# Cross attention in a perceiver: transposes issued one step earlier, remainders subtracted in pieces by GpSimd, small vector work moved to ScalarE

## The chip, the cores and the metric

The kernel runs on one core of one Trainium2 chip. The time is the device time of one execution in microseconds. A core has TensorE (PE, with PEld as its weight load), VectorE (DVE), ScalarE (ACT), GpSimd (POOL) and SyncE (SP, which issues the DMAs); each works through its own queue in order and waits on semaphores.

## The reference, cut to what matters

The network has twelve stages on `x` of (2, 256, 256), that is 512 rows of 256. Stages 0, 3 and 6 are cross attentions with one head of width 256 against a context of (2, 4096, 256); the others (self attentions, feed forwards, and a 16-head cross attention as stage 9) are not touched.

```python
h = layernorm(x)
q = (h @ Wq + bq) * scale
scores = q @ (ctx @ Wk + bk).T          # stage 0: masked keys count as -inf
p = softmax(scores)                     # over 4096 keys
x = x + (p @ (ctx @ Wv + bv)) (@ Wo + bo in stage 0)
```

The kernel uses that `q Wk^T` can be formed once (512 x 256), so that scores are products with the context itself, and that the value weights can be applied after the mixing. `c = q . bk` is added to each row of scores.

## The kernel before, in words

`xattn(s, ...)` (L556 on) builds the programs of the four compute engines for the three cross attentions; `masked` is true for stage 0 alone, `project` too. The 512 rows are 4 tiles of 128 (`tile_of`), the 4096 keys of a batch are 4 parts of 1024, each part two chunks `k` of 512. A **step** `g` (0 to 15) is one tile against one part; its halves `h` are its two chunks. Steps `2j` and `2j+1` share their chunks, so a chunk is used by two steps one after the other.

The products keep the accuracy of float32 with three products of a narrower type: each operand is split into a head (`copy` to fp32r) and a remainder (operand minus head). What is split for every chunk:
- the transposed context: head `cth(k)` by ACT (`split_t`, L838), remainder `ctr(k)` by a subtraction (`rest_of_context`, L684) of 128 x 1024. `ctr_by_pool` says who does it: POOL for chunks 2 to 15 in stage 0, DVE for everything in stages 3 and 6;
- the context: head `cnh(k)` by ACT (`split_n`, L842), remainder `cnr(k)` by POOL (L897, 128 x 1024).

A step on TensorE: `score(g, h)` is 6 products of 512 columns (L163, in `mm`), `turn(g, h)` 4 transposes (L632) of the exponentials `P`, `mix(g, h)` 12 products of 256 columns (L163). The order is written out by hand: `turn(g,0)`, `score(g+2,0)`, `turn(g,1)`, `mix(g,0)`, `score(g+2,1)`, `mix(g,1)`; after step 13 the turns and mixes of steps 14 and 15, then the transposes of the result (L346, L347), the value product and the output product.

DVE in a step: in stage 0 `masked_scores` (L730: scores + c, min with a bound `MB` that `bound` builds from mask bytes, L722) for each half; `largest` (L737 a reduction over 1024 columns, then on 128 x 1 values L743/L746/L749 the running maximum, L753/L756 its negative `nb`, L758 the `gap` to the maximum before); `add_mixed` (L782, L785, L789); `sums` (L766 and, for a tile's last part, L770, L772, L774); `rest_of_weights` (L795: the transposed exponentials minus their head); in stages 3 and 6 `rest_of_context`.

ACT in a step: `head_of_weights(g, 0)` (L847), `exp(g+1)` (L852 on 128 x 1 from the gap, L854 on 1024 columns), `head_of_weights(g, 1)`, `split_t(g+4)`, `split_n(g+2)`.

POOL: in stages 3 and 6 first the key jobs of stage 9 (`job_pool`, L474 to L480, four instructions of 512 columns for one job; two jobs in `b3`, four in `b6`), then `split_t(2)`, `split_n(0)`, `split_t(3)`, `split_n(1)` (each `split_t` only where POOL has it), the jobs `t3`/`t6` (one each), `add_row_pool` (L364, four additions of 128 x 256), then for k from 2 on `split_t(k+2)`, `split_n(k)`.

Buffers: heads and remainders of the context rotate through 3, exponentials `P` through 2, `PTH`/`PTR` (transposed exponentials) through 3, the banks of the turns through 2 (`TR`; `TE`, with two banks of the scores, for steps 14 and 15).

At the start of a stage PE makes `q` (2 x 4 products), then `c` (24 products of one column in all with `bk`), then `q2 = Wk q` whose head `qnh` ACT takes (L871) and whose remainder `qnr` DVE (L709); `score(0, 0)` waits for `qnr` and `ctr(0)`.

## Time and profile before

| what | us |
| --- | --- |
| median of 3 runs (lowest, highest) | 1529.64 (1528.77, 1535.45) |
| the profiled execution, its own time | 1532.3 |
| its span in the profile | 1530.3 |
| busy: PE, DVE, ACT, POOL | 1439.8, 972.8, 739.3, 307.2 |
| mean granted clock of TensorE | 0.988 |

The span is the time from the first to the last instruction in the profile; the execution's own time is 2.0 us more. A granted clock of 1.0 is 2.4 GHz, 0.5 is 1.2 GHz. In the rows, a time at the left is the start in us from the span's start, the next number the duration; what stands in square brackets is the engine's idle time just before and what ended it. A row of windows has the stretch, its length, then the busy time of PE, PEld, DVE, ACT and POOL with the number of instructions, the granted clock, and DMA's share and GB/s. A busy PE row ends by a model, so start-to-start distances are used for TensorE. The three cross attentions lie at about 0 to 171, 383 to 519 and 610 to 747 us.

### The profile page before, as it was taken

To read this page: it belongs to the slowest core of one execution; us is meant where nothing else is said; L and a number is where in the kernel's file an instruction comes from. 1 tells how busy PE (TensorE), PEld (TensorE's weight loads), DVE (VectorE), ACT (ScalarE), POOL (GpSimd) and SP (SyncE) were. 2 spreads that over 40 slices of the span, in tenths; PEclk is the share of its full clock that TensorE was granted. 3 is DMA by queue.
4 is the path that set the end of the run, shared out by engine and by line. 5 is a ranking of instruction groups with operands and counts; after the bars stand their busy time and mean duration, and the time that the engine had idled before them with its cause. 6 is when DMAs were issued, how large, how long until landed. Compare 5 with 4: busy or idle time off the path is not lost.

```text
span 1530.3 us, 26042 instructions
## 1 busy us (share of the span) xinstructions
PE 1439.8 (94%) x10503; PEld 986.9 (64%) x10513; DVE 972.8 (64%) x1714; ACT 739.3 (48%) x1363; POOL 307.2 (20%) x253
## 2 busy tenths in 40 slices
PE   7888999999999899899899999999999899999998
PEld 4777574888688665689655544555555454555697
DVE  5787465454677454677454258889999892566533
ACT  3554333111566333566353246777777677315232
POOL 1665231000733040933202050110000000100000
PEclk9999999999999999999999999999999999999999
DMA  9311324221120520210313366654776611410140
GB/s 374 118 56 52 152 79 142 70 95 61 42 81 28 229 81 8 72 71 28 129 30 121 130 135 134 93 82 69 136 153 118 113 22 61 200 56 1 49 172 14
DMA packets 43005, 147.72 MB, mean 97 GB/s; under 512 B 6380, under 2 KB 21996, under 8 KB 34028
## 3 DMA queue, kind: packets, MB, share of 16 engines
q1 hardware_dynamic: 42888, 146.07, 33.2%
q8 instruction: 84, 1.38, 0.4%
q14 instruction: 33, 0.27, 0.1%
HBM read 123.49 MB, written 22.56 MB: 95 GB/s over the span
## 4 chain that ended last, share of the span: by engine, by line
PE 78%; DVE 9%; ACT 3%; issue 2%; ACTq 0%; DVEq 0%
PE PS L163 47%; PE PS L2363 8%; PE PS L2275 7%; PE PS L2260 5%; PE PS L1624 2%; PE PS L632 2%; DVE SM L2379 2%; PE PS L1853 1%; PE PS L1874 1%; DVE SM L737 1%; PE PS L2354 1%; PE PS L2949 1%; PE PS L1881 1%; PE PS L2854 1%; DVE AR L1068 0%
## 5 line engine op out<-in xcount | busy, mean ns | idle before, releaser
L2379 DVE TENSOR_REDUCE SM<-PS 128x1 f32<-128x1024 f32 x256 | 301.6, 1219 | 38.4 <-PE PS L2260 37.3
L163 PE MATMUL PS<-ARr 128*128 128x256 f32 (+1 forms) x672 | 172.8, 323 | 20.8 <-DVE ARr L795 11.1
L2275 PE MATMUL PS<-AR 49*128 49x256 bf16 (+1 forms) x1216 | 162.5, 271 | 1.1 <-DVE AR L2400 0.7
L163 PE MATMUL PS<-HT,AR 128*128 128x512 f32 x328 | 152.7, 613 | 2.5 <-ACT HT L355 1.6
L163 PE MATMUL PS<-CNr,ARr 128*128 128x256 f32 x672 | 129.5, 290 | 12.8 <-DVE ARr L795 8.1
L163 PEld LDWEIGHTS PS<-ARr 128*128 128x128 f32 x672 | 117.4, 194 | 35.4 <-issue 14.5
L163 PE MATMUL PS<-ARr,HTr 128*128 128x512 f32 x384 | 127.3, 413 | 4.1 <-DVE ARr L684 3.0
L2275 PE MATMUL PS<-AR,CT 49*128 49x256 bf16 (+1 forms) x832 | 124.2, 271 | 0.0
L163 PEld LDWEIGHTS PS<-CNr,ARr 128*128 128x128 f32 x672 | 103.0, 195 | 18.1 <-issue 8.2
L847 ACT CAST ARr<-PS 128x512 fp32r<-128x512 f32 x96 | 56.0, 583 | 121.4 <-PE PS L632 120.1
L163 PEld LDWEIGHTS PS<-HT,AR 128*128 128x128 f32 x328 | 61.1, 194 | 77.5 <-issue 73.6
L163 PE MATMUL PS<-AR 128*128 128x256 f32 (+3 forms) x504 | 109.7, 372 | 1.4 <-DVE AR L701 0.8
L2452 ACT ACTIVATE AR<-PS 128x512 f32<-128x512 f32 x172 | 93.5, 602 | 25.7 <-PE PS L2275 25.7
L2452 ACT ACTIVATE CT<-PS 128x512 f32<-128x512 f32 x168 | 91.5, 602 | 24.4 <-PE PS L2275 24.3
L163 PEld LDWEIGHTS PS<-AR 128*128 128x128 f32 x504 | 89.5, 190 | 19.2 <-issue 6.6
L474 POOL CAST CN<-CN 128x512 bf16<-128x512 f32 x32 | 20.3, 635 | 379.0 <-ACT HT L355 208.4
L2275 PEld LDWEIGHTS PS<-AR 49*128 49x128 bf16 (+1 forms) x1216 | 81.2, 94 | 20.2 <-issue 7.0
L163 PE MATMUL PS<-CT,CN 128*128 128x512 f32 (+1 forms) x256 | 89.8, 490 | 1.1 <-ACT AR L2465 1.1
L163 PE MATMUL PS<-CN,CT 128*128 128x256 f32 (+1 forms) x448 | 85.5, 340 | 2.4 <-DVE AR L1070 0.8
L897 POOL TENSOR_TENSOR CNr<-CN,ARr 128x1024 fp32r<-128x1024 f32 x30 | 70.3, 2344 | 70.3 <-ACT ARr L842 70.3
L163 PEld LDWEIGHTS PS<-CN,CT 128*128 128x128 f32 x448 | 70.5, 192 | 20.5 <-issue 10.3
L795 DVE TENSOR_TENSOR ARr<-PS,ARr 128x512 fp32r<-128x512 f32 x96 | 65.6, 687 | 25.5 <-ACT ARr L847 24.9
(397 smaller groups left out, 2708.6 us busy)
## 6 DMA issues: line engine op xcount, KB each, us to landing
CN<-ctx_n SPq DMA_DIRECT2D x24, 1024.0 KB, 5.0
AR<-k_parts SPq DMA_DIRECT2D x114, 128.0 KB
k_parts<-CN SPq DMA_DIRECT2D x32, 384.0 KB, 3.4
CT<-pack SPq DMA_DIRECT2D x6, 2048.0 KB, 8.0
AR<-pack SPq DMA_DIRECT2D x20, 512.0 KB, 4.6
CT<-k_parts SPq DMA_DIRECT2D x78, 128.0 KB
CT<-ctx_t SPq DMA_DIRECT2D x8, 1024.0 KB, 18.8
v_ones<-CN SPq DMA_DIRECT2D x28, 288.0 KB, 3.3
```

Source lines behind the costliest of these rows:

```text
L163: last = te.matmul(o, l, r, start=first and k == 0, stop=final and k == n - 1, skip_group_check=True)
L474: ge.tensor_copy(p[:, 0, :], r).then_inc(*pl.inc("split", "p0", 9, n))
L632: z = te.transpose(PS[:, b, tok(y)], P[g % 2][:, tok(4 * h + y)], ident)
L795: ve.tensor_tensor(PTR[u % 3], bank("pt", s, g, h), PTHf[u % 3], ALU.subtract).then_inc(*dv.inc("turn", "ptr", s, g, h))
L847: ae.copy(PTH[u % 3], bank("pt", s, g, h)).then_inc(*ac.inc("turn", "pth", s, g, h))
L897: pl.e.tensor_tensor(context_n(k, CNr), context_n(k, CN), CNHf[k % 3], ALU.subtract).then_inc(*pl.inc("rest", "cnr", s, k))
L1624: z = te.matmul(ACC[i], h[:, tok(i)], W[f"d{e}"], start=e == 0 and i % 2 == 0, stop=e == n - 1, skip_group_check=True)
L2260: return te.matmul(PS[:, b + y, :], QQ9[M_ROWS[e], pr, 0, tok(2 * b2 + g % 8 // 4)], KM9[g // 8 % 4][M_ROWS[e], c * 512:c * 512 + 512], st ...
L2275: return te.matmul(PS[:, b, z * 256:z * 256 + 256], keys[rows, c * 128:c * 128 + 128], QQ9[rows, pr, rest, cols], start=not rest, stop=boo ...
L2363: z = te.matmul(PS[32 * y:32 * y + 32, 7, 0:256], VP9[:, 2 * s + y % 2, 17 * h:17 * h + 32], PT9[n % 6][:, y, :], start=s == 0, stop=s == ...
L2379: ve.tensor_reduce(MX9[:, p % 2, e, g % 8 // 4, g % 4:g % 4 + 1], PS[:, b:b + 2, :].rearrange("p a b -> p (a b)"), AX, ALU.max).then_inc(* ...
L2452: ae.activation(PT9[i % 6][:, 2 * e:2 * e + 2, :], bank("st", 9, p, s, e).rearrange("p (c q) -> p c q", c=2), ACT.Exp).then_inc(*ac.inc("e ...
```

## The change

On TensorE, `turn(g+1, 0)` is issued ahead of `mix(g, 1)`, with the same order down to the last step, and the transposes of the result are issued tile by tile between the last mixes; in stages 3 and 6 the output products of tiles 0 and 1 stand ahead of the transposes of tile 3. The products `q2` come ahead of `c`. On DVE the running maximum is kept in an array `top`, so that in stage 0 it is a reduction over two neighbours instead of a two-operand maximum; the gap is gone, and ACT takes the exponential of the difference of the two maxima with its scale and bias. `bound` moves from DVE to ACT. `sums` moves behind `largest`. On ACT the context heads 0 and 1 are made ahead of `qnh`, and the order within a step is `head_of_weights(g, 1)`, `exp(g+1)`, `split_t(g+4)`, `bound(g+4)`, `head_of_weights(g+1, 0)`, `split_n(g+2)`. On POOL each subtraction of 1024 columns becomes four of 256, and `ctr(k)` for k from 2 on is POOL's in all three stages.

```diff
...
-        TE = banks.ring((4,), (5,), (0,), (2,))
+        OR = banks.ring((0,), (1,), (2,), (3,))
...
-            mxc, mx, nb, gap, al, rs, tot = (sm(16) for _ in range(7))
+            low = sm(1)
+            top = sm(4, 5, 2)
+            nb, al, rs, tot = (sm(16) for _ in range(4))
...
-            ctr_by_pool = lambda k: masked and k > 1
+            ctr_by_pool = lambda k: k > 1
...
+                for m in range(2):
+                    b, before = PB.take(("q2", s, m), ("qnr", s, m))
+                    pe.wait_ge(*before, ("qt", s, 0), ("qt", s, 1))
+                    mm(te, PS[:, b, :], [(Wk[:, h, tok(m)], QT[:, h, :]) for h in range(2)]).then_inc(
+                        *pe.inc("proj", "q2_ps", s, m))
                 b, before = PB.take(("c", s), ("cadd", s))
-                pe.wait_ge(*before, ("qt", s, 0), ("qt", s, 1))
+                pe.wait_ge(*before)
                 for i in range(4):
                     z = mm(te, PS[:, b, i:i + 1], [(QT[:, m, tok(i)], W["bk"][:, m:m + 1]) for m in range(2)])
                 z.then_inc(*pe.inc("proj", "c_ps", s))
-                for m in range(2):
-                    b, before = PB.take(("q2", s, m), ("qnr", s, m))
-                    pe.wait_ge(*before)
-                    mm(te, PS[:, b, :], [(Wk[:, h, tok(m)], QT[:, h, :]) for h in range(2)]).then_inc(
-                        *pe.inc("proj", "q2_ps", s, m))
                 if s:
                     half_pe(pe, f"h{s}", 1)
 
...
                 def turn(g, h):
-                    b, before = (TR if g < 14 else TE).take(("pt", s, g, h), ("ptr", s, g, h))
+                    b, before = TR.take(("pt", s, g, h), ("ptr", s, g, h))
                     pe.wait_ge(*before, ("e", s, g))
...
+                def turn_mixed(i):
+                    b, before = OR.take(("ot", s, i), ("ot", s, i))
+                    pe.wait_ge(*before, ("o", s, i))
+                    te.transpose(PS[:, b, 0:128], OB[:, i, 0:128], ident)
+                    te.transpose(PS[:, b, 128:256], OB[:, i, 128:256], ident).then_inc(*pe.inc("turned", "ot_ps", s, i))
+
...
                 for g in range(2):
                     score(g, 0)
                     score(g, 1)
-                for g in range(14):
-                    turn(g, 0)
-                    score(g + 2, 0)
+                turn(0, 0)
+                for g in range(16):
+                    if g < 14:
+                        score(g + 2, 0)
                     turn(g, 1)
                     mix(g, 0)
-                    score(g + 2, 1)
+                    if g < 14:
+                        score(g + 2, 1)
+                    if g < 15:
+                        turn(g + 1, 0)
+                    else:
+                        turn_mixed(0)
+                        turn_mixed(1)
                     mix(g, 1)
-                turn(14, 0)
-                turn(14, 1)
-                mix(14, 0)
-                turn(15, 0)
-                mix(14, 1)
-                turn(15, 1)
-                mix(15, 0)
-                mix(15, 1)
-                turn_all(pe, s, "ot", OB, "o")
-                src, Wf, ready = OT, Wv, [("ot", s, i) for i in range(4)]
+                turn_mixed(2)
                 if project:
+                    turn_mixed(3)
                     for m in range(2):
                         b, before = PB.take(("v", s, m), ("cx", s, m))
-                        pe.wait_ge(*before, *ready)
+                        pe.wait_ge(*before, *[("ot", s, i) for i in range(4)])
                         mm(te, PS[:, b, :], [(Wv[:, kt, tok(m)], OT[:, kt, :]) for kt in range(2)]).then_inc(
                             *pe.inc("proj", "v_ps", s, m))
-                    src, Wf, ready = CX, mat(W["Wo"], 2), [("cx", s, m) for m in range(2)]
-                for i in range(4):
-                    b, before = PB.take(("y", s, i), ("x", s, i))
-                    pe.wait_ge(*before, *ready)
-                    mm(te, PS[:, b, 0:256], [(src[:, kt, tok(i)], Wf[:, kt, :]) for kt in range(2)]).then_inc(
-                        *pe.inc("proj", "y_ps", s, i))
+                    for i in range(4):
+                        product(i, CX, mat(W["Wo"], 2), ("cx", s, 0), ("cx", s, 1))
+                else:
+                    product(0, OT, Wv, ("ot", s, 0))
+                    product(1, OT, Wv, ("ot", s, 1))
+                    turn_mixed(3)
+                    product(2, OT, Wv, ("ot", s, 2))
+                    product(3, OT, Wv, ("ot", s, 3))
                 pe.end(s)
 
...
                 pr.wait_ge(("cth", s, k))
-                pr.e.tensor_tensor(CTR[k % 3], context_t(k), CTHf[k % 3], ALU.subtract).then_inc(
-                    *pr.inc("rest", "ctr", s, k))
+                for kt, c in pieces or [(slice(0, 2), slice(0, 512))]:
+                    z = pr.e.tensor_tensor(CTR[k % 3][:, kt, c], context_t(k)[:, kt, c], CTHf[k % 3][:, kt, c],
+                                           ALU.subtract)
+                z.then_inc(*pr.inc("rest", "ctr", s, k))
...
-                if not masked:
+                if masked:
+                    ve.memset(low, -BIG).then_inc(*dv.inc("fill", "low"))
+                else:
                     rest_of_context(dv, 0)
...
-                dv.wait_ge(("c_ps", s))
-                ve.tensor_copy(cadd, bank("c", s)[:, 0:4]).then_inc(*dv.inc("proj", "cadd", s))
-                if not masked:
-                    rest_of_context(dv, 1)
+                if masked:
+                    rest_of_context(dv, 0)
+                rest_of_context(dv, 1)
                 for m in range(2):
                     dv.wait_ge(("qnh", s, m))
                     ve.tensor_tensor(QNR[:, m, :], bank("q2", s, m), QNHf[:, m, :], ALU.subtract).then_inc(
                         *dv.inc("proj", "qnr", s, m))
-                if masked:
-                    rest_of_context(dv, 0)
-                    rest_of_context(dv, 1)
-                else:
-                    rest_of_context(dv, 2)
-
-                def bound(g, h):
-
-                    k = chunk_of(g, h)
-                    c = slice(k % 8 * 512, k % 8 * 512 + 512)
-                    dv.wait_ge(("mu", g // 8), ("s", s, *last_use(k - 8)) if k > 7 else None)
-                    ve.tensor_scalar(MB[:, c], MU[g // 8][:, c], 2 * BIG, -BIG, ALU.mult, ALU.add).then_inc(
-                        *dv.inc("bound", "bound", k))
-
+                dv.wait_ge(("c_ps", s))
+                ve.tensor_copy(cadd, bank("c", s)[:, 0:4]).then_inc(*dv.inc("proj", "cadd", s))
...
-                            ve.scalar_tensor_tensor(out=of(mx, g), in0=of(mxc, g), scalar=c, in1=of(mx, g - 2), op0=ALU.add,
-                                                    op1=ALU.max).then_inc(*dv.inc("largest", "mx", s, g))
+                    ve.tensor_reduce(top[:, i, n, 1:2], P[g % 2] if masked else scores(g), AX, ALU.max).then_inc(
+                        *dv.inc("largest", "mxc", s, g))
+                    dv.wait_ge(("mxc", s, g), ("mx", s, g - 2) if n else None)
+                    if masked:
+                        ve.tensor_reduce(top[:, i, n + 1, 0:1], top[:, i, n, 0 if n else 1:2], AX, ALU.max).then_inc(
+                            *dv.inc("largest", "mx", s, g))
+                    elif n == 0:
+                        ve.tensor_scalar(top[:, i, 1, 0:1], top[:, i, 0, 1:2], c, None, ALU.add).then_inc(
+                            *dv.inc("largest", "mx", s, g))
+                    else:
+                        ve.scalar_tensor_tensor(out=top[:, i, n + 1, 0:1], in0=top[:, i, n, 1:2], scalar=c,
+                                                in1=top[:, i, n, 0:1], op0=ALU.add, op1=ALU.max).then_inc(
+                            *dv.inc("largest", "mx", s, g))
                     dv.wait_ge(("mx", s, g))
                     if masked:
...
-                    if not first:
-                        ve.tensor_tensor(of(gap, g), of(mx, g - 2), of(mx, g), ALU.subtract).then_inc(
-                            *dv.inc("largest", "gap", s, g))
+                        ve.tensor_tensor(of(nb, g), c, top[:, i, n + 1, 0:1], ALU.subtract).then_inc(
+                            *dv.inc("largest", "nb", s, g))
 
...
-                for g in range(16):
+                rest_of_weights(0, 0)
+                for g in range(15):
                     if g:
                         add_mixed(g - 1)
-                    sums(g)
-                    rest_of_weights(g, 0)
-                    if masked and g + 2 < 16:
+                    if masked and g < 14:
                         masked_scores(g + 2, 0)
                     rest_of_weights(g, 1)
                     if g + 4 < 16 and not ctr_by_pool(g + 4):
                         rest_of_context(dv, g + 4)
-                    if g + 2 < 16:
-                        if masked:
-                            masked_scores(g + 2, 1)
+                    if masked and g < 14:
+                        masked_scores(g + 2, 1)
+                    rest_of_weights(g + 1, 0)
+                    if g < 14:
                         largest(g + 2)
+                    sums(g + 1)
+                add_mixed(14)
+                rest_of_weights(15, 1)
...
                 add_mixed(15)
+                turn_mixed(2)
...
-                turn_out(dv, s, "ot", OT, 0)
...
-                    ac.wait_ge(("pt_ps", s, g, h), ("mix", s, (u - 3) // 2, (u - 3) % 2) if u > 2 else ("q2_ps", s, 1))
+                    ac.wait_ge(("pt_ps", s, g, h), ("mix", s, (u - 3) // 2, (u - 3) % 2) if u > 2 else ("c_ps", s))
...
-                        ac.wait_ge(("gap", s, g))
-                        ae.activation(of(al, g), of(gap, g), ACT.Exp).then_inc(*ac.inc("exp", "al", s, g))
+                    i, n = tile_of(g), part_of(g)
+                    if n:
+                        ac.wait_ge(("mx", s, g))
+                        ae.activation(of(al, g), top[:, i, n + 1, 0:1], ACT.Exp, scale=-1.0, bias=top[:, i, n, 0:1]).then_inc(
+                            *ac.inc("exp", "al", s, g))
                     ac.wait_ge(("nb", s, g), ("pt_ps", s, g - 2, 1) if g > 1 else None)
...
+                def bound(k):
+
+                    c = slice(k % 8 * 512, k % 8 * 512 + 512)
+                    ac.wait_ge(("mu", k // 8), ("low",), ("s", s, *last_use(k - 8)) if k > 7 else None)
+                    ae.activation(MB[:, c], MU[k // 8][:, c], ACT.Identity, scale=2 * BIG, bias=low).then_inc(
+                        *ac.inc("bound", "bound", k))
...
+                split_t(0)
+                split_t(1)
                 if s:
-                    split_t(0)
-                    split_t(1)
...
-                    for k in range(3):
-                        split_t(k)
+                    for k in range(4):
+                        bound(k)
+                    split_t(2)
                 split_n(0)
-                split_n(1)
                 exp(0)
                 split_t(3)
-                for g in range(16):
-                    head_of_weights(g, 0)
-                    if g + 1 < 16:
-                        exp(g + 1)
+                split_n(1)
+                head_of_weights(0, 0)
+                for g in range(15):
                     head_of_weights(g, 1)
+                    exp(g + 1)
                     if g + 4 < 16:
                         split_t(g + 4)
+                        if masked:
+                            bound(g + 4)
+                    head_of_weights(g + 1, 0)
                     if g + 2 < 16:
                         split_n(g + 2)
-                turn_out(ac, s, "ot", OT, 1)
+                head_of_weights(15, 1)
+                turn_mixed(1)
+                turn_mixed(3)
                 end_act(ac, s)
 
...
-                    pl.e.tensor_tensor(context_n(k, CNr), context_n(k, CN), CNHf[k % 3], ALU.subtract).then_inc(
-                        *pl.inc("rest", "cnr", s, k))
+                    for y in range(4):
+                        z = pl.e.tensor_tensor(context_n(k, CNr)[:, y, :], context_n(k, CN)[:, y, :], CNHf[k % 3][:, y, :],
+                                               ALU.subtract)
+                    z.then_inc(*pl.inc("rest", "cnr", s, k))
 
                 def split_t(k):
                     if ctr_by_pool(k):
-                        rest_of_context(pl, k)
+                        rest_of_context(pl, k, *[(kt, c) for kt in range(2) for c in (slice(0, 256), slice(256, 512))])
...
```

In the parts left out, `largest` writes the raw maximum of part n to `top[:, i, n, 1]`, `product` is the old output product, and `turn_mixed` on DVE and ACT is the old copy of the transposed result for one tile.

## Rows read from the trace of the kernel before

**Rows 1.** Windows from turn(0,0) or turn(2,0) to turn(14,0) in stages 0, 3, 6

```profile
36.50:148.18 111.68, 95.74 (x614) 84.79 (x613) 87.89 (x150) 58.71 (x94) 69.36 (x32) 0.97 0.19 68
419.60:499.95 80.35, 79.48 (x527) 70.93 (x525) 60.91 (x108) 49.96 (x80) 28.74 (x13) 1.00 0.16 54
648.70:728.66 79.96, 78.92 (x523) 70.76 (x521) 59.23 (x108) 49.08 (x80) 25.78 (x13) 1.00 0.17 56
```

**Rows 2.** Chain that ended last, stage 0, one step (start, us, what)

```profile
126.21 1.53 DVE SM L746
```

**Rows 3.** Groups of instructions by form, 44 to 149 us

```profile
L847 ACT CAST ARr<-PS 128x512 fp32r<-128x512 f32 x27 | 15.6, 576 | 33.4 <-PE PS L632 33.3
...
L746 DVE TENSOR_TENSOR SM<-SM 128x1 f32<-128x1 f32 x11 | 13.2, 1199 | 0.4
...
L722 DVE TENSOR_SCALAR CN<-CN 128x512 bf16<-128x512 uint8 x12 | 6.5, 545 | 0.0
```

**Rows 4.** Timeline, stage 0, POOL, DVE and PE around 44 to 50 us

```profile
44.19 2.38 POOL L684 TENSOR_TENSOR ARr<-CT,ARr 128x1024 fp32r<-128x1024 f32 x1
...
44.67 1.91 DVE L746 TENSOR_TENSOR SM<-SM 128x1 f32<-128x1 f32 x1
...
46.52 2.34 POOL L897 TENSOR_TENSOR CNr<-CN,ARr 128x1024 fp32r<-128x1024 f32 x1
...
46.69 2.19 DVE L758 TENSOR_TENSOR SM<-SM 128x1 f32<-128x1 f32 x1
...
49.86 2.93 PE L163 MATMUL PS<-CNr,ARr 128*128 128x256 f32 x12 [3.60 <-DVE ARr L795]
```

**Rows 5.** Timeline of PE, stage 3: a mix, and the second transposes behind it

```profile
431.10 1.59 PE L163 MATMUL PS<-CNr,ARr 128*128 128x256 f32 x12
...
434.35 0.60 PE L632 MATMUL PS<-CST,AR 128*128 128x128 f32 x4
```

**Rows 6.** Timeline, start of stage 0

```profile
17.59 5.49 PE L163 MATMUL PS<-AR 128*128 128x1 f32 x24 [0.84 <-DVE AR L701]
...
26.05 1.19 PE L163 MATMUL PS<-ARr,HTr 128*128 128x512 f32 x2 [2.97 <-DVE ARr L684]
...
26.95 2.61 DVE L722 TENSOR_SCALAR CN<-CN 128x512 bf16<-128x512 uint8 x1
...
35.74 1.11 PE L632 MATMUL PS<-CST,AR 128*128 128x128 f32 x4 [2.60 <-ACT AR L854]
```

**Rows 7.** DMA issues from 2.6 to 2.7 us (last number: us to landing)

```profile
CT<-ctx_t SPq DMA_DIRECT2D x1, 1024.0 KB, 10.6
```

**Rows 8.** PE after step 13, stage 3, with a window inside, then stage 0

```profile
503.12 0.37 PE L163 MATMUL PS<-ARr 128*128 128x256 f32 x1 [2.14 <-issue]
...
504.00:505.00 1.00, 1.00 (x7) 1.00 (x6) 0.00 (x0) 0.00 (x0) 0.00 (x0) 0.50 0.99 418
...
510.37 0.35 PE L163 MATMUL PS<-ARr 128*128 128x256 f32 x1 [1.74 <-DVE ARr L795]
...
515.01 3.69 PE L163 MATMUL PS<-AR,HT 128*128 128x256 f32 x16 [0.55 <-ACT HT L355]
...
163.29 3.67 PE L163 MATMUL PS<-HT,AR 128*128 128x512 f32 x8 [0.55 <-ACT HT L355]
...
167.80 3.72 PE L163 MATMUL PS<-AR,H 128*128 128x256 f32 x16 [0.85 <-DVE H L827]
```

**Rows 9.** Timeline of POOL (one of ACT) at the start of stages 0, 3, 6

```profile
41.63 2.59 POOL L364 TENSOR_TENSOR X<-X,AR 128x256 f32<-128x256 f32 x4
...
402.64 0.61 POOL L474 CAST CN<-CN 128x512 bf16<-128x512 f32 x1 [0.16 <-POOL CNr L897]
...
403.64 1.03 ACT L838 CAST ARr<-CT 128x1024 fp32r<-128x1024 f32 x1
...
407.25 3.86 POOL L364 TENSOR_TENSOR X<-X,AR 128x256 f32<-128x256 f32 x4
...
630.98 2.38 POOL L897 TENSOR_TENSOR CNr<-CN,CNr 128x1024 fp32r<-128x1024 f32 x1
```

37 lines of the change are left out of this document (18 added, 19 removed).

## The prediction

> **What bounds the kernel now.** I read the page first, then windows over the three cross attentions, because nothing outside them is edited. From turn to turn a step takes 111.68/14 = 7.98 us in stage 0, but 80.35/12 = 6.70 in stage 3 and about 6.7 in stage 6 [rows 1]. TensorE's work is the same in all three. From the start of a mix to that of the second set of transposes behind it (a mix, a set and a score, no gap) 434.35 - 431.10 = 3.25 us pass, and that is half a step: 6.50 [rows 5]. I work with **6.53**, split by columns: a score (6 x 512) 1.39, a mix (12 x 256) 1.41, transposes (4 x 128) 0.47 where they stand clear. So stage 0 has 1.45 us a step to give, stages 3 and 6 only 0.17.
>
> Who takes it in stage 0 is in the chain: DVE's running maximum on 128 x 1 values (L746) stands in it, with 1.53 us in the step shown [rows 2]. Over the loop it takes 1.20 on average, for one element a partition, [rows 3]. The timeline shows why: POOL starts a subtraction at 44.19 that ends at 46.57, and DVE's two-operand instruction from 44.67 ends at 46.58. The next one starts at 46.69 and ends at 48.88, with POOL's next subtraction, which ends at 48.86; TensorE then stands 3.60 us [rows 4]. A DVE instruction with two operands in SBUF waits for the whole POOL instruction in flight. The bound from bytes (L722), one operand of 512 columns, suffers the same: 2.61 us at the start, 0.55 on average [rows 3, 6].
>
> **Part 1, the loop of stage 0.** The new order puts turn(g+1,0) ahead of mix(g,1). Call T the start of a step on TensorE: score(g+2,0) to T+1.39, turn(g,1) to 1.86, mix(g,0) to 3.27, score(g+2,1) to 4.66, turn(g+1,0) to 5.13, mix(g,1) to 6.53. The wait that is added is turn(g+1,0)'s for exp(g+1), and mix(g,1) is queued behind it. ACT: head(g,1) ends at about 2.65, the exponential with its small one 4.04; due at 4.66, so 0.6 to spare. Then the transposed head (5.0), bound (5.5), head(g+1,0) (6.1). DVE: remainder 6.7, reduction 8.0, maximum and negative 8.4, which is T'+1.9 in the next step, ahead of ACT's 2.65 there. DVE's sums and the addition of the mix end by T'+3.2 even with one 0.65 wait, the second remainder at 4.6, due at 5.13. The loop closes on TensorE with 0.5 to spare.
>
> Loads: DVE had 87.89 us in 14 steps; without L746 and L722 it is 68.2, 4.9 a step, plus a reduction of two elements [rows 1, 3]. ACT had 4.2 a step and gets bound; nothing shows that on ACT, the nearest is its 512-column copy, 0.58 [rows 3]; below nothing is excluded, above I keep 1.1. That makes 4.8. POOL had 69.36/14 = 4.95; four 256-column additions took 2.59, so a unit of four pieces is 2.6 to 2.7 against 2.38 whole, and two units 5.4 a step [rows 1, 4, 9]. The upper end is 3.86 for such a four, while DVE was using the same side [rows 9]. All under 6.53. I price a step at **6.60**, between 6.53 and the 6.70 of stage 3.
>
> **Part 2, the start of stage 0.** q2 now follows qt directly, at 17.6, and c (1.9 us of one-column products within the 5.49 of the row) comes behind it [rows 6]. q2 ends at 21.05 and c at 22.95; both remainders are done by 22.6. The context heads 0 and 1 go ahead of qnh on ACT's queue, but the first 1 MB, issued at 2.7, lands at 13.3, in ACT's idle time: cost nothing; if it were after 19.5 it would hold qnh up one for one [rows 7]. The first score moves from 26.05 to 23.0. Four scores end at 28.6 at full clock (before they began at half clock after a 2.97 idle). The bounds, on ACT from 21.8 to 24.2, no longer stop DVE for 2.61. exp(0) ends at 29.5, turn(0,0) starts at 29.6 against 35.74 [rows 6]. Step 0 then waits 0.9 for head and remainder, so step 1 starts at 37.6 (37.5 on the side of POOL: cnr(1) 36.1). Step 14: 37.6 + 13 x 6.60 = 123.4. Before it is 148.18 + 0.47 = 148.65. **-25.2.**
>
> **Part 3, the loops of stages 3 and 6.** ctr(k) leaves DVE, which doesn't bind there. On POOL it is a second unit of 2.7. In steady state 5.4 of 6.6 is enough, and ctr(g+4) is ready 1.8 us before its score. But POOL starts with a debt. In stage 3, ctr(3) can't start before the head at 403.7; then come ctr(3), cnr(1), the job (402.64 to 407.25, 4.6), the row additions (2.7), ctr(4), cnr(2), ctr(5), cnr(3): 6 units, 403.7 + 16.2 + 4.6 + 2.7 = 427.2 [rows 9]. mix(2,1) needs cnr(3), so step 3 starts at 428.6 where TensorE could be at 423.9. Step 14: 428.6 + 11 x 6.60 = 501.2, against 499.95 + 0.47 = 500.4 [rows 1]: **+0.8.** In stage 6 four jobs hold POOL until 630.98; ctr(2), which DVE made beside them, now stands first, and with cnr(0), ctr(3), cnr(1), the row additions, ctr(4), cnr(2), ctr(5), cnr(3) it makes nine units, beside a job: 631.0 + 24.3 + 4.6 = 659.9, step 3 at 661.3, step 14 at 733.9 against 729.1 [rows 1, 9]: **+4.8.** ctr(2) at 633.7 keeps score(2,0) waiting some 3 us there; that lies inside this sum. The 0.6 us won at each start by c behind q2 is lost in the debt.
>
> **Part 4, the ends.** Before, from the end of turn(14,0) TensorE stood 2.14 us, ran three us at half clock (1.2 GHz granted in the window from 504), stood 1.74, mixed until 513.3, transposed four tiles, stood 0.55 and made the products until 518.6: 18.2 us from 500.4 [rows 8]. Now: turn(14,1), mix(14,0) to T+1.9; turn(15,0) waits for exp(15) until 3.3 and ends 3.8; mix(14,1) 5.2, turn(15,1) 5.7, mix(15,0) 7.1, two tiles' transposes 7.5, mix(15,1) 9.0 (its remainder is there at 7.6), tile 2 at 9.25, two products of 0.92 to 11.1, tile 3 11.35, products to 13.2. **-5.0** in stage 3 and, with the same shape, in stage 6. In stage 0, 22.75 (to 171.4) becomes 9.2 + 1.6 + the 8.1 of value and output products = 18.9: **-3.9** [rows 8]. A 1.4 us stall remains where there was 2.14; the clock fell after the 2.14 and not after the 1.74, so I count full clock. The bound on the other side is 1.3 each.
>
> **Sum.** -25.2 + 0.8 + 4.8 - 5.0 - 5.0 - 3.9 = -33.5 against the profiled execution's own 1532.3: 1498.8. That execution stands 2.7 above the median of 1529.64, so the median to expect is **1496**.
>
> Two rules beside it. GpSimd's subtraction of 1024 columns took 2.38 [rows 4]. The Trainium skill (GPSIMD Engine Reference, 3.1 Elementwise) gives 4.5 us for 2048 columns, which as an estimate is 0.56 for a 256 piece; with it the 16 units of debt would come to some 7 us less and the sum to 1489; the row has 2.38 for half of that and wins. The skill (Perfetto Trace Analysis, Optimizing Scalar/DVE Operations) also warns that moving work between these two engines may not help since they share a port; that speaks against part 3 and is rival C below.
>
> **The rivals.**
> A. *The debt is larger.* If the pieces stretch to the 3.86 per four that the row additions took beside DVE [rows 9], but only while POOL works without a break, each of 16 units costs 1.2 more: +19, 1515. Halfway, 1506. For it: DVE's small two-operand work is still there in stages 3 and 6. Against: the 2.59 of stage 0.
> B. *The turned-ahead wait binds.* If bound on ACT or a late maximum eats more than the 0.6, by say 0.5, stage 0 pays 14 x 0.5 = 7: 1503.
> C. *The pieces don't give way.* If DVE has to let all four pieces pass, it waits 2.6 for L766 and, in stages 3 and 6, up to three times; steps go back to about 7.9 in stage 0 and the gain is what ends and start give, 14 + 6, less the debt: about 1520 to 1528. Against: DVE got in at 46.58 between two POOL instructions that followed each other [rows 4]. The Trainium skill (SBUF, State Buffer, SBUF: two separate sides) gives the port to whoever starts first for a whole instruction, which leaves open who is first after a piece.
> D. *Slower.* POOL becomes the bound in all three loops. It decides above 6.6/8 = 0.825 us a piece; at the 0.96 of 3.86/4 a step takes 7.72, 1.12 more for 13 + 11 + 11 steps, +39, with A's 19: 1554.
> E. *Better.* Steps at 6.53 and a piece of 0.6: -2.5 - 4: 1489.
>
> **How the numbers follow.** Forecast 0.58, A 0.17, B 0.09, C 0.05, D 0.03, E 0.08. The range from 1487 to 1510 holds the forecast, E, B and half of A. Half a per cent, about what can be told here, is 7.6 us: faster means under 1522. C is half in that band: faster 0.93, same 0.04, slower 0.03.
>
> **What would show it.** Steps of stage 0 at 6.5 to 6.7 start to start, no DVE instruction on 128 x 1 above 0.8, a POOL piece of 0.65; turn(0,0) near 30; in stages 3 and 6 TensorE waiting in step 2 for POOL's L684 and L897, in stage 6 also ahead of score(2,0), and 6.6 afterwards; the end of each stage about 13 us (stage 0: 19) from the last score's step. It is wrong if TensorE waits for L854 in every step, or if POOL has no gap left by step 8.

## The result, and the profile after

The changed kernel takes **1511.24 us** (median of 4 runs, 1508.56 to 1514.65) against 1532.21 for the kernel before on the same chip (a fourth run moved its median from the 1529.64 of the table): ratio **0.9865**, 95% interval 0.9831 to 0.9898. It is faster, by 21 us or 1.35%, clear of the spread of the runs. The forecast was a fall of 33.5 us to 1496, and the time lies above its range, which ended at 1510. The profiled execution took 1511.16 with a span of 1509.4, 20.9 less than the 1530.3 before.

In the changed kernel the lines have moved: L700 and L929 are POOL's remainders of the transposed and the plain context, L364 the row additions, L747 the masked maximum of two values, L753 and L761 the unmasked maximum and its negative, L769 the running sum of the softmax, L634 the transposes of the weights, L798 their remainder.

Where the 20.9 us come from is read at landmarks: instructions on TensorE or ACT that stand at the same place in both programs. First the kernel before: the first value product after stage 0, ACT's copies ahead of the queries of stages 3 and 6, the first transposes of stage 4, the first product of stage 7, the last wait near the end.

```profile
384.49 0.63 ACT L355 COPY HT<-PS 128x256 f32<-128x256 f32 x2
540.40 0.33 PE L346 MATMUL PS<-CST,AR 128*128 128x128 f32 x1 [0.42 <-ACT AR L1515]
611.89 0.63 ACT L355 COPY HT<-PS 128x256 f32<-128x256 f32 x2
755.59 7.11 PE L163 MATMUL PS<-HT,AR 128*128 128x512 f32 x16 [0.43 <-ACT HT L355]
1522.06 1.13 PE L2946 MATMUL PS<-CN 128*128 128x256 f32 x4 [1.13 <-ACT CN L3180]
```

The same in the changed kernel, with its end of stage 0 (before: 163.29, [rows 8]):

```profile
142.63 3.67 PE L163 MATMUL PS<-HT,AR 128*128 128x512 f32 x8 [0.55 <-ACT HT L886]
363.07 0.63 ACT L355 COPY HT<-PS 128x256 f32<-128x256 f32 x2
515.61 0.33 PE L346 MATMUL PS<-CST,AR 128*128 128x128 f32 x1 [0.43 <-ACT AR L1548]
587.10 0.63 ACT L355 COPY HT<-PS 128x256 f32<-128x256 f32 x2
731.23 7.10 PE L163 MATMUL PS<-HT,AR 128*128 128x512 f32 x16 [0.43 <-ACT HT L355]
1501.15 1.13 PE L2979 MATMUL PS<-CN 128*128 128x256 f32 x4 [1.13 <-ACT CN L3213]
```

Row by row the shift is -20.66, -21.42, -24.79, -24.79, -24.36 and -20.91. So:

| part | forecast | measured |
| --- | --- | --- |
| stage 0 | -29.1 | -20.7 |
| stages 1, 2 | 0 | -0.8 |
| stage 3 (loop, end) | -4.2 (+0.8, -5.0) | -3.4 (+0.6, -3.9) |
| stage 6 (loop, end) | -0.2 (+4.8, -5.0) | +0.4 (+1.0, -0.6) |
| behind stage 6 | 0 | +3.5 |

Of the 12.5 us between forecast and measurement, 8.4 are in stage 0 and 3.5 in a part of the program that the change doesn't touch. Stage 6 is within 0.6 of its forecast only because two errors of about 4 us cancel, in its loop and in its end.

**Stage 0.** The loops as in [rows 1], here from step 1 to turn(14,1) in stage 0 and over parts of the loops of stages 3 and 6:

```profile
35.49:129.62 94.13, 86.78 (x574) 77.98 (x573) 72.65 (x120) 60.13 (x98) 70.96 (x102) 0.96 0.24 86
418.94:479.88 60.94, 60.71 (x414) 54.76 (x413) 43.86 (x69) 38.45 (x61) 47.70 (x68) 1.00 0.12 39
645.00:707.00 62.00, 62.00 (x426) 56.35 (x424) 41.39 (x70) 39.03 (x62) 43.30 (x70) 1.00 0.14 47
```

Stages 3 and 6 have TensorE busy throughout. Stage 0 has 7.35 us of TensorE idle in 94.13, and 7.32 of them are one wait. The timeline of POOL, DVE and PE around it (PE's first row is turn(3,0), its second mix(2,1)):

```profile
22.70 2.84 POOL L700 TENSOR_TENSOR ARr<-CT,ARr 128x256 fp32r<-128x256 f32 x4 [22.26 <-ACT ARr L850]
...
33.81 2.43 POOL L364 TENSOR_TENSOR X<-X,AR 128x256 f32<-128x256 f32 x4
...
44.55 2.85 POOL L929 TENSOR_TENSOR CNr<-CN,CNr 128x256 fp32r<-128x256 f32 x4
...
50.04 2.81 POOL L929 TENSOR_TENSOR CNr<-CN,ARr 128x256 fp32r<-128x256 f32 x4
...
43.61 9.26 DVE L769 SCALAR_TENSOR_TENSOR SM<-SM 128x1 f32<-128x1 f32 x1
...
46.59 0.60 PE L634 MATMUL PS<-CST,AR 128*128 128x128 f32 x4
54.51 2.93 PE L163 MATMUL PS<-CNr,ARr 128*128 128x256 f32 x12 [7.32 <-DVE ARr L798]
```

The reader is to see two ends: POOL works from 22.70 without an idle interval and ends at 50.04 + 2.81 = 52.85; DVE's instruction on one element a partition, begun at 43.61, ends at 52.87. It has let not one piece pass but all that were left, 13 of them. Behind it on DVE stands the remainder L798 for which TensorE waits; and after the stall the mix runs at half clock (granted 0.50 from 54.5), 2.93 instead of 1.65. Step 3 begins at 57.24; from steps 1 and 2 at 35.49 and 41.95 it would have been 48.4. That is 8.8 us lost, and step 3, still in part at half clock, costs 0.8 more. Since the start was 2.1 better than forecast and the other steps a little shorter, step 14 comes 6.2 us after its forecast (129.62 for 123.4). Elsewhere the pieces give way: from 64.54 to 129.62 ten steps take 6.51 each.

The same in small, in stage 3, at the end of POOL's first run there (407.70 + 2.86 = 410.56; DVE ends at 410.58), with the waits of step 2 that the prediction named:

```profile
396.76 0.73 PE L163 MATMUL PS<-ARr,HTr 128*128 128x512 f32 x2 [1.27 <-POOL ARr L700]
399.61 0.36 PE L163 MATMUL PS<-ARr 128*128 128x256 f32 x1 [0.77 <-POOL CNr L929]
402.28 0.74 PE L163 MATMUL PS<-ARr,HTr 128*128 128x512 f32 x2 [1.01 <-POOL ARr L700]
405.13 1.66 PE L163 MATMUL PS<-CNr,ARr 128*128 128x256 f32 x12 [0.74 <-POOL CNr L929]
...
407.70 2.86 POOL L929 TENSOR_TENSOR CNr<-CN,ARr 128x256 fp32r<-128x256 f32 x4
...
406.90 3.68 DVE L753 SCALAR_TENSOR_TENSOR SM<-SM 128x1 f32<-128x1 f32 x1
```

**Behind stage 6.** In stage 9, TensorE waits for "issue", nothing that the profile shows, in the middle of a mix. Three rows of the changed kernel have no counterpart before; two others (2.48 and 1.93) stand in both.

```profile
1078.68 0.41 PE L2396 MATMUL PS<-AR,CN 128*32 128x256 f32 x2 [1.12 <-issue]
...
1108.48 0.40 PE L2396 MATMUL PS<-CT,CN 128*32 128x256 f32 x1 [1.85 <-issue]
...
1128.46 0.64 PE L2396 MATMUL PS<-HT,CN 128*32 128x256 f32 x8 [1.74 <-issue]
```

### The profile page after: what moved, and what is told of

Read it like the earlier page. It is cut to its first block, busy times and chain, and to the rows that moved or that the text cites. A ratio compares the mean times of both kernels' runs of the same rounds, so it can differ in the third digit from the quotient of the medians.

```text
span 1509.4 us, 26305 instructions
## 1 busy us (share of the span) xinstructions
PE 1430.7 (95%) x10513; PEld 979.5 (65%) x10513; DVE 939.3 (62%) x1639; ACT 750.0 (50%) x1379; POOL 397.7 (26%) x551
## 4 chain that ended last, share of the span: by engine, by line
PE 79%; DVE 10%; POOL 4%; ACT 4%; issue 3%; DMA 0%; SPq 0%; POOLq 0%; ACTq 0%; DVEq 0%
PE PS L163 48%; PE PS L2396 8%; PE PS L2308 7%; PE PS L2293 5%; PE PS L634 2%; PE PS L1657 2%; DVE SM L2412 2%; POOL ARr L700 1%; PE PS L1886 1%; POOL CNr L929 1%; PE PS L1907 1%; DVE SM L743 1%; PE PS L2387 1%; PE PS L2982 1%; PE PS L1914 1%
## 5 line engine op out<-in xcount | busy, mean ns | idle before, releaser
L163 PE MATMUL PS<-ARr 128*128 128x256 f32 (+1 forms) x672 | 177.3, 323 | 2.3 <-POOL CNr L929 2.0
L700 POOL TENSOR_TENSOR ARr<-CT,ARr 128x256 fp32r<-128x256 f32 x168 | 113.4, 710 | 65.8 <-ACT ARr L850 65.8
L163 PE MATMUL PS<-ARr,HTr 128*128 128x512 f32 x384 | 122.5, 400 | 4.7 <-POOL ARr L700 4.2
L798 DVE TENSOR_TENSOR ARr<-PS,ARr 128x512 fp32r<-128x512 f32 x96 | 65.9, 687 | 77.6 <-ACT ARr L859 77.3
L929 POOL TENSOR_TENSOR CNr<-CN,ARr 128x256 fp32r<-128x256 f32 x120 | 81.0, 712 | 9.3 <-ACT ARr L854 9.3
```

The lines of the kernel that those rows point to most:

```text
L163: last = te.matmul(o, l, r, start=first and k == 0, stop=final and k == n - 1, skip_group_check=True)
L700: z = pr.e.tensor_tensor(CTR[k % 3][:, kt, c], context_t(k)[:, kt, c], CTHf[k % 3][:, kt, c], ALU.subtract)
L798: ve.tensor_tensor(PTR[u % 3], bank("pt", s, g, h), PTHf[u % 3], ALU.subtract).then_inc(*dv.inc("turn", "ptr", s, g, h))
L929: z = pl.e.tensor_tensor(context_n(k, CNr)[:, y, :], context_n(k, CN)[:, y, :], CNHf[k % 3][:, y, :], ALU.subtract)
```

## The experiments

The time of each kernel is a median of 4 or more runs, and its ratio, with its 95% interval, is to the kernel before on the chip of that run. Kernels 5, 9 and 12 ran once, for their traces alone. Unless another is named, a kernel is the changed one with the edit shown.

**1. The changed kernel again.** No edit.

> The changed kernel once more, not edited. Its first profile has two things that the sum did not have: in stage 0 one DVE instruction on 128 x 1 values (L769) takes 9.26 us, to 52.87, the moment at which POOL's first unbroken run of pieces ends (52.85), and TensorE stands 7.32 us; and between 1054 and 1144 us TensorE stands three times (1.12, 1.85, 1.74 us) with nothing that the profile names. If the 9.26 is how two engines in a fixed order meet, it is there again at the same place, within 0.5 us of the end of POOL's run. If it was an accident of that execution, no instruction of L769 is above 3 us in this one. The three nameless waits: if they belong to the program, they return at the same instructions; if they are an accident, some are missing and the span is shorter by their sum, up to 4.7 us.

1509.34 us, ratio 0.9845 (0.9812 to 0.9877). L769 at 43.58 takes 9.22; L753 takes 3.70 in stage 3 and 2.87 in stage 6, as in the first profile. The stall belongs to the program. Of the three nameless waits two are back at the same instructions (1.58 and 1.19), the third is not there, at least not above 0.6.

**2. The running sum on ACT.**

```
-  dve: ve.scalar_tensor_tensor(out=of(tot, g), in0=of(tot if n > 1 else rs, g - 2), scalar=of(al, g), in1=of(rs, g), ...)
+  act, behind head_of_weights(g + 1, 0):
+       ae.activation(of(tot, g), of(tot if n > 1 else rs, g - 2), ACT.Identity, scale=of(al, g), bias=of(rs, g))
```

> The sums' running total (L769, three operands in SBUF) is computed on ACT, behind the transposed head of the next step; nothing else moves, POOL's run of pieces is the same. Theory H (DVE is held for as long as POOL works without a gap, as soon as all operands of its instruction lie in SBUF): stage 0 has no such instruction left inside POOL's first run, TensorE's 7.32 us stall and the half clock behind it go, step 3 starts at 48.4 instead of 57.2, and the time is 8 to 9 us below the changed kernel's 1511: 1502 to 1503. Rival P (POOL's late start itself, 11 units without a gap, is what TensorE waits for, and L769 only happens to end with it): the wait moves to a remainder of L700 or L929 and at least 5 of the 8.8 us remain: 1507 to 1511. If ACT's order becomes the bound instead, turn(g+1,0) shows a wait for L868 in every step.

**1495.06 us**, ratio 0.9755 (0.9729 to 0.978). The stall is gone and nothing took its place; PE in stage 0, then at its end:

```profile
47.65 1.61 PE L163 MATMUL PS<-CNr,ARr 128*128 128x256 f32 x12 [0.35 <-POOL CNr L934]
...
120.30 0.60 PE L634 MATMUL PS<-CST,AR 128*128 128x128 f32 x4
...
123.22 0.66 PE L634 MATMUL PS<-CST,AR 128*128 128x128 f32 x4 [0.90 <-ACT AR L865]
124.28 1.65 PE L163 MATMUL PS<-CNr,ARr 128*128 128x256 f32 x12 [0.41 <-DVE ARr L795]
...
131.18 3.67 PE L163 MATMUL PS<-HT,AR 128*128 128x512 f32 x8 [0.55 <-ACT HT L890]
```

turn(14,1) is at 120.30 instead of 129.62, and stage 0 ends 11.4 us earlier. Rival P, POOL's late start itself, had room for 0.35. The 2.1 beyond the stall are in the end: from turn(14,1) to the value product it took 13.01 in the changed kernel and takes 10.88 here, since the remainder ahead of mix(14,1) comes after 0.41 and not 0.90 and that mix takes 1.65 and not 2.88. The medians are 14 us apart on this chip (1509.3 and 1495.1), the profiled spans 17.7 (1509.4 and 1491.7). Of these 17.7, 11.4 are stage 0 and 4.1 the part from the first product of stage 9 to the last landmark, where the nameless waits are: it takes 616.4 here and 620.5 in the changed kernel.

**3. POOL waits for itself ahead of every unit; 4. POOL's subtractions whole.**

```
   # 3: in split_n(k), and in split_t(k) for k > 2, ahead of the pieces
+  pl.wait_last()
   # 4: in split_n and split_t
-  four pieces of 256 columns, the increment on the last
+  pl.e.tensor_tensor(<1024 columns>, ALU.subtract).then_inc(...)
```

> POOL waits for the completion of its own last piece ahead of every unit of four pieces, so that a short gap (estimate 0.05 to 0.2 us) stands between two units; all else as in the changed kernel. Theory H, with a gap of any length enough: no DVE instruction with its operands in SBUF takes longer than a unit, 2.9 us, so L769 falls from 9.26 to under 2.9, TensorE's stall from 7.32 to about 1, and the time to about 1505, less the gaps' cost of 11 x 0.1 = 1. Rival G (the gap must be a real idle of POOL, as when it waits for ACT): the 9.26 stays or grows with the longer run to about 10, time 1511 to 1513.

> POOL's subtractions whole again, 1024 columns by one instruction, the new order and all of them on POOL kept: one part of the change undone. Theory H1 (what holds DVE back is any run of POOL without a gap, whatever the size of its instructions): L769 still waits until the run's end, about 8 us. Theory H2 (only short POOL instructions that follow each other hold DVE back; at the end of a whole one it gets in, as at 46.58 in the kernel before): no DVE instruction on 128 x 1 takes more than 2.5 us, the 7.32 us stall goes to about 1.5, stage 0's steps become longer by one such wait in some of them, and the time is between 1502 and 1512. POOL's unit is 2.4 instead of 2.83, so its run in stage 0 ends some 4 us earlier in both cases.

Kernel 3: 1501.81 us, 0.9803 (0.9775 to 0.9831); L769 at 44.22 takes 0.71 and no instruction on 128 x 1 is over 1.3. Gaps of 0.08 and 0.14 us between units are enough. Yet DVE got in at 44.93, at the end of the third piece of a unit and not in a gap (POOL's unit runs from 42.78 to 45.61), so the gap works by something else than by being open.

```profile
42.78 2.83 POOL L700 TENSOR_TENSOR ARr<-CT,ARr 128x256 fp32r<-128x256 f32 x4
...
44.22 0.71 DVE L769 SCALAR_TENSOR_TENSOR SM<-SM 128x1 f32<-128x1 f32 x1
```

Kernel 4: 1502.99 us, 0.9809 (0.978 to 0.9839): by the medians, undoing the pieces is worth 6 us against kernel 1 on the same chip, with intervals that just overlap. Its instructions on 128 x 1 wait for POOL's instruction in flight, 2.42 us at most:

```profile
43.45 2.39 POOL L928 TENSOR_TENSOR CNr<-CN,CNr 128x1024 fp32r<-128x1024 f32 x1
...
44.24 1.62 DVE L769 SCALAR_TENSOR_TENSOR SM<-SM 128x1 f32<-128x1 f32 x1
```

Theory H as I had written it (any work without a gap holds DVE out) falls with this one; H2 (only short instructions do) stands for now. POOL's longest run without a gap has 11 instructions here, which kernel 12 will show to matter.

**5. The two engines alone; 9. the same, phase swept.** New kernels that compute nothing of the reference: POOL subtracts constant tiles, DVE reduces from PSUM and then does one instruction like L769.

> Not the reference's computation at all: only the two engines beside each other, on constant tiles, in ten stretches. POOL makes six units of 1024 columns; DVE makes eight pairs of a reduction from PSUM (256 to 928 columns, to shift the phase) and one instruction on 128 x 1 values with three operands in SBUF. The stretches: 1 and 2 pieces of 256 columns, the increment on the last of four only; 3 pieces with an increment on each; 4 whole subtractions of 1024; 5 pieces with POOL waiting for itself after each unit; 6 the same after each piece; 7 halves of 512; 8 POOL idle; 9 pieces, DVE's instruction with one operand in PSUM and 512 columns; 10 pieces, DVE's instruction a maximum of two values, one operand. Theory H (no entry while POOL works without a gap): in 1, 2, 3 and 7 the first small instruction lasts until POOL's run is over, 10 us or more, in 4 too. Theory Q (it gets in at the end of POOL's instruction with a chance that depends on the phase): in 1, 2, 3 most wait 0.1 to 0.8 us, and a few wait several pieces; in 4 up to 2.4; in 5 and 6 never longer than the way to the next gap. 8 and 10 give about 0.2 for both, 9 its 0.7, unless an operand in PSUM does not free it.

> Again only the two engines on constant tiles, not the reference's computation. 132 trials: POOL makes 16 pieces of 256 columns without a pause; DVE reduces 1024 to 1712 columns from PSUM, in steps of 16 (0.017 us each, so 44 steps go once round a piece of 0.68), and then comes one instruction on 128 x 1 values with three operands in SBUF. First 44 trials: the reduction directly ahead. Next 44: a one-operand instruction on 128 x 1 between the two, as L758 stands ahead of L769. Last 44: the same, and POOL asks a semaphore that has long been reached ahead of each unit. Theory S (a window of phase): the instruction gets in at the next boundary (at most 0.8 us) except where it arrives in a narrow window of phase, and there it stays out until POOL's run ends, 6 to 8 us; few trials, next to each other. Theory Q: it arrives too late for one boundary and gets the next, at most 1.4 us in every trial; then the 9.26 of the changed kernel has a condition that these trials don't have. If only the second or third group has long ones, that group's difference is the condition.

In kernel 5 no stretch has an instruction kept out: pieces 0.21 to 0.78, whole units up to 2.06, halves up to 1.36; with POOL idle 0.21; an operand in PSUM 0.74 and one operand 0.14 to 0.15, both undisturbed. In kernel 9 all 132 trials are between 0.21 and 0.79, and go round with the phase. Theories H and S are both wrong. What these trials lack is depth: DVE came at most 9.3 us, 14 pieces, into a run, while L769 came in the 31st.

**6. Transposed remainders of stages 3 and 6 back on DVE; 7. one operand; 8. rows late.** 6 and 7 stand on kernel 2, 8 on 7.

```
   # 6
-  ctr_by_pool = lambda k: k > 1
+  ctr_by_pool = lambda k: masked and k > 1
   # 7: unmasked as masked: the maximum without c, which falls out of the softmax
+  ve.tensor_reduce(top[:, i, n + 1, 0:1], top[:, i, n, 0 if n else 1:2], AX, ALU.max)
+  ve.tensor_scalar(of(nb, g), top[:, i, n + 1, 0:1], -1.0, None, ALU.mult)
   # 8: in pool_part, moved from ahead of the loop
   for k in range(2, 16):
+      if k == 10:
+          add_row_pool(...)
```

> The sums on ACT as in the kernel before it (1495.1), and in stages 3 and 6 the transposed context's remainders back on DVE: one part of the change undone. Theory D (POOL's late start in these stages is a cost of the change): the four waits of step 2 for L700 and L929, 3.8 us in stage 3 and about 3.3 in stage 6, go; DVE's own subtraction (1.24 for 1024 columns in one instruction, all operands in SBUF) comes into each step and holds it no longer than a POOL piece. Expected 1495.1 - 3.8 - 3.3 + about 1 for DVE's waits: 1488 to 1491. Rival: DVE's 1024 columns, all in SBUF, are held back by POOL's pieces for several us in some steps, steps go to 6.7 and above, and the gain is eaten: 1494 to 1500.

> As with the sums on ACT, and in stages 3 and 6 the maximum is taken of the scores without the constant of the query row, which falls out of a softmax: L753 and L761, with all operands in SBUF, are replaced by the maximum of two values and a product with -1, as in stage 0. DVE then has no small instruction with two operands in SBUF in the loops but one in four parts. Theory H or Q: the 3.7 and 2.9 us of L753 at the end of POOL's run go; they stand in front of exp(4), so TensorE's wait of 0.6 there and a little at the end of each stage go: 1 to 3 us less, 1492 to 1494. Rival N (these waits were hidden): no change, 1495.

> As the one before, and POOL adds the rows to X in the middle of the loop, ahead of the unit for chunk 10, where it idles, not before the loop. Theory D: POOL's start is shorter by its 2.4 to 2.8 us in stages 3 and 6, so that of TensorE's 3.8 and 3.3 us of waits in step 2 about 2.5 go in each: 1487 to 1490, 5 below the one before. In stage 0 it only takes off 0.3 (a wait for L929). Rival: the additions in the loop push two units past their due times and TensorE waits there instead: no gain.

1491.35 (0.9756, 0.9722 to 0.979), 1492.47 (0.9757, 0.9718 to 0.9796) and 1490.58 (0.9751, 0.9715 to 0.9786): against kernel 2's 0.9755 none of the three is told apart from it by its whole time. The profiles do tell them apart. From turn(0,0) of stage 3 to the first transposes of stage 4 the changed kernel takes 135.0, kernel 2 134.3, kernel 6 130.4, kernel 7 132.6, kernel 8 129.9. So POOL's late start in stage 3 costs 4 us, as theory D said: the remainders on DVE give back 3.9, the late rows 2.7 and the one operand 1.7. But the part behind the first product of stage 9 takes 622.5 in kernels 6 and 8, 6 us more than in kernel 2: TensorE's "issue" waits there sum to 8.5 and 7.6 for 4.5, its other waits are 1 us more, and the rest of it is in its busy time. The gain is there and is lost again at a place that no edit touches.

**10. All four edits.**

> The four edits that helped together: sums on ACT, maximum without the row's constant in stages 3 and 6, row additions inside the loop, and the transposed context's remainders of stages 3 and 6 back on DVE. From the profiles, stage by stage: stage 0 as with the sums on ACT; stage 3 at least as short as the shorter of the two before it (130.4 with the remainders on DVE, 129.9 with late rows, from turn(0,0) to stage 4's first transposes), estimate 128.5 since TensorE's wait for L929 in step 2 and 0.5 us at the end go too; stage 6 likewise, its wait of 2.07 for L929 gone. Expected 2 to 3 us below the 1490.6 of late rows, if stage 9's nameless waits are the same: 1488. Rival: DVE's 1024 columns, all in SBUF, get held back by POOL's pieces now that the row additions stand in the loop, and nothing is gained: 1490 to 1492.

**1483.90 us** (5 runs, 1480.08 to 1489.83), ratio 0.9685 (0.9659 to 0.9711): faster than both kernels, by 3.2% than the one before. Stage 3's stretch is 127.7. One wait for POOL of some size is left, 2.25 us for L924 in stage 6.

**11. The pieces alone, in the kernel before.** Old order, old placement.

> The kernel before with one part of the change alone: POOL's subtractions in pieces of 256 columns; the old order, the transposed remainders of stages 3 and 6 on DVE. The prediction's reasoning: L746 on 128 x 1, 1.20 us on average, falls to at most a piece, about 0.5, so stage 0's steps go from 7.98 to 7.3 or so, less what POOL's unit costs more: 14 x 0.6 = 8 us, 1522 against 1530. Theory H or S (pieces in an unbroken run can hold DVE out for several us): one or more of L746, L756, L766 last 3 us or more inside POOL's first run, 22 to 50 us, and take part of it back: 1524 to 1530.

1529.18 us (10 runs), ratio 0.9985 (0.9966 to 1.0004): no gain that can be told. Stage 0 ends 3.6 us earlier (159.71 against 163.29), and the part behind the first product of stage 9 takes 3.4 more (620.3 against 616.9), with the nameless waits that the kernel before has not. So these waits need neither the new order nor POOL's extra work. And this stands in stage 0; the timelines of POOL, DVE and PE:

```profile
49.78 2.81 POOL L685 TENSOR_TENSOR ARr<-CT,ARr 128x256 fp32r<-128x256 f32 x4
52.55 2.75 POOL L900 TENSOR_TENSOR CNr<-CN,CNr 128x256 fp32r<-128x256 f32 x4
...
43.15 0.49 DVE L760 TENSOR_TENSOR SM<-SM 128x1 f32<-128x1 f32 x1
...
50.80 4.52 DVE L748 TENSOR_TENSOR SM<-SM 128x1 f32<-128x1 f32 x1
...
56.74 0.55 PE L163 MATMUL PS<-ARr 128*128 128x256 f32 x1 [4.33 <-DVE H L784]
```

50.80 + 4.52 = 55.32, POOL's run ends at 55.30. The starvation comes with the pieces and not with the new order. L748 came in the 22nd instruction of that run; in the same run L748 and L760 had got in at 42.68 and 43.15, after 0.37 and 0.49, in the 10th and 11th. So an entry of DVE doesn't set the run back: only 11 POOL instructions lie between the one that let DVE in and the one that doesn't. The changed kernel's stage 3 has the same, L769 in at 398.03 after 0.77, in the 11th, and L753 kept out in the 24th of 29.

**12. Depth.** Engines alone, runs of about 30 us, one arrival of DVE in each, ever later.

> The two engines alone again, constant tiles, not the reference's computation: runs of POOL of about 30 us (12 units), and one DVE instruction on 128 x 1 values with three operands in SBUF in each, after 1, 3, 5 ... 23 reductions of 1.2 us, so 1 to 28 us into the run. Four groups of 12: quarters (pieces of 256 columns, no gap), units (the same, POOL waits for itself after each four), halves (512 columns), whole (1024). Theory L (depth): in the full kernels the instructions that were kept out came 20 or more pieces into an unbroken run (43.58, 407.2, 635.5, and 50.8 in the old order), those that came up to 11 pieces in got in at the next boundary. If depth is the condition, in quarters every instruction behind some depth between 14 and 21 pieces (10 to 14 us) waits until the run ends, 15 to 20 us for the first such, and units shows none. Halves and whole then tell time from count: by time, from 10 to 14 us on as well; by count, halves only from 17 us on and whole never. Rival: every one gets in at the next boundary at any depth (0.8, 0.8, 1.3 and 2.5 us at most); then depth is not the condition and it stays open.

DVE's row in the fourth, fifth and sixth run of pieces; those runs begin at 102.57, 135.49 and 168.59:

```profile
110.45 0.34 DVE L54 SCALAR_TENSOR_TENSOR SO<-SM 128x1 f32<-128x1 f32 x1
145.63 22.55 DVE L54 SCALAR_TENSOR_TENSOR SO<-SM 128x1 f32<-128x1 f32 x1
180.82 20.47 DVE L54 SCALAR_TENSOR_TENSOR SO<-SM 128x1 f32<-128x1 f32 x1
```

and of halves, runs from 1018.83 and 1048.39:

```profile
1035.76 0.21 DVE L54 SCALAR_TENSOR_TENSOR SO<-SM 128x1 f32<-128x1 f32 x1
1067.58 10.14 DVE L54 SCALAR_TENSOR_TENSOR SO<-SM 128x1 f32<-128x1 f32 x1
```

This is the cause, and it is a count. A piece follows the next in 0.68 us: 7.88 us into the run, in the 12th, DVE gets in; 10.14 us in, in the 15th, it waits 22.55 us, to the end of the run at 168.17. All eight arrivals from there on end with their run. Halves follow in 1.22 us: 16.93 us in, in the 14th, it gets in, 19.19 us in, in the 16th, it is out until the run ends, as are the next three. With a wait of POOL for itself after each four, which leaves gaps of 0.08 us, twelve arrivals at up to 26 us all take 0.62 or less. Whole units, twelve to a run, are waited for one at a time, 1.64 at most; no trial has 15 of them in a row. It isn't the number of columns either: 14 halves have more columns than 15 pieces. In kernel 5 an arrival in the 14th piece still got in, after 0.28. So from the 15th instruction of POOL that follows the others without a gap, DVE's instruction isn't let in between them. Which part of the engine counts, the rows can't say.

**13. Two waits; 14. the control.** Whether the count decides in the full kernel too.

```
   # 13: in split_t(k)            # 14: in split_t(k)
+  if k in (4, 6):              +  if k in (3, 9):
+      pl.wait_last()           +      pl.wait_last()
```

> The changed kernel with two short waits of POOL for its own last piece, ahead of the transposed remainders of chunks 4 and 6, in each of the three stages; nothing else. Theory N (count): DVE is kept out only once 15 or 16 instructions of POOL have followed each other without a gap. With the waits, L769 at 43.6 comes 11 pieces after one, and L753 in stages 3 and 6 comes 3 or 4 after one: none of them takes longer than 0.8 us, TensorE's 7.3 us stall goes, and the time is that with a wait at every unit or a little less (about 28 gaps of 0.18 us fewer, some of them under the debt): 1500 to 1502. Rival: only a wait at every unit helps, the 9.2 us are there again.

> The control: as many waits, of the same kind, but ahead of chunks 3 and 9, so that in stage 0 L769 at 43.7 comes 23 pieces after one. Theory N: it is kept out again until POOL's run ends at about 53, for some 9 us; L753 in stages 3 and 6 as in the changed kernel; time as the changed kernel, 1509 to 1512. Rival (any wait early in the run resets what keeps DVE out): no long instruction, 1501.

Kernel 13: **1499.48 us**, 0.9802 (0.9777 to 0.9826), no instruction on 128 x 1 over 1.3. Kernel 14: 1509.75 us, 0.9861 (0.9842 to 0.9881), the time of the changed kernel. The first row below is from kernel 13, where POOL's last gap, of 0.08 us, ended at 37.78 and the row comes in the 11th piece behind it; the second, in a fence of its own, from kernel 14, in the 23rd piece behind the gap:

```profile
45.06 0.44 DVE L769 SCALAR_TENSOR_TENSOR SM<-SM 128x1 f32<-128x1 f32 x1
```

```profile
45.25 9.20 DVE L769 SCALAR_TENSOR_TENSOR SM<-SM 128x1 f32<-128x1 f32 x1
```

As many waits of the same kind, 10 us of difference by where they stand, and the two intervals lie apart.

**15. All four edits with whole subtractions.** Kernel 10 with kernel 4's edit.

> The four edits together (1483.9), and POOL's subtractions whole, 1024 columns by one instruction, as in the kernel before. DVE's small instructions no longer need both operands from SBUF in the loops, so pieces have nothing to give way to; a whole unit takes 2.4 instead of 2.83. Stage 0's wait of 0.5 for cnr(1) goes; in stages 3 and 6 DVE's own 1024 columns may now wait up to 2.4 for POOL in the steps in which they meet, which has 0.5 to 1 us of room. If the room is enough: 1482 to 1483.5. If not, steps of stages 3 and 6 go to 6.7 and the time to 1485 to 1488.

1486.00 us, ratio 0.9715 (0.9696 to 0.9734) against 0.9685 (to 0.9711): by the medians the pieces are worth some 2 to 4 us in the best version, at the edge of what can be told. The landmarks agree: the first product of stage 9 comes at 857.10 and in kernel 10 at 853.65, 3.5 earlier, while the part behind it is 4.7 shorter here (618.3 and 623.0), again where no edit is. The steps are as long as with pieces (6.5), so the forecast of longer ones was wrong; half of the 3.5 is at the end of stage 0. There the product L762 of two values, the only small instruction of DVE left with two operands in SBUF, takes 1.35 at 122.64, and the mix at 125.44 takes 2.20 after a wait of 0.93, where kernel 10 has 1.66 after 0.39.

## Why the prediction was wrong

**The step that failed** is the dismissal of rival C, "the pieces don't give way". I argued it away with one case, DVE getting in at 46.58 between two POOL instructions [rows 4], and took that for a rule at any depth. In the kernel before nothing contradicts it: its longest run of POOL without a gap has 8 instructions. The change multiplies the number of subtractions by four and gives POOL a debt at the start of a stage, which I had worked out myself, for stages 3 and 6, to be an unbroken run; its longest runs have 44 instructions in stage 0 and 29 in stages 3 and 6, and L769 comes in the 31st. What C names does happen, but in one place a stage and not in every step. In stage 0 it costs 8.8 us, between my forecast and C's price; without it (kernels 2 and 13) the time is 1495 to 1499 and inside the range. C's price was itself not worked out: its terms as written, 14 + 6 less a debt of 5.6, give 1515, and the rest up to 1528 would have to come from waits in stages 3 and 6 that it names but doesn't add up. The pieces did give way in every later step, runs of two units being 8 instructions long.

Point by point:
- *Start of stage 0*: score(0,0) at 20.15 (forecast 23.0), turn(0,0) 26.93 (29.6), step 1 at 35.49 (37.6). Right in kind, and 2.1 us better at step 1. The one-column products behind q2 overlap the remainders more than I gave them.
- *Steps*: 6.51 to 6.54 in all three stages where nothing starves; forecast 6.60. (The 7.98 of the kernel before leaves out its first set of transposes; with it the step was 8.01.) The wait of turn(g+1,0) for the exponential binds once in the three loops, 0.65 at 412.07, behind the kept-out L753: rival B is out. Bound on ACT takes 0.72, forecast 0.58 within bounds of 0 and 1.1. POOL's unit takes 2.83 and not 2.7; it idles in every step behind the start, so rival D is out, and the 3.86 of rival A is not seen.
- *Debt in stages 3 and 6*: stage 3's loop +0.6 (forecast +0.8), with the waits in step 2 on the lines named. Stage 6's +1.0 against +4.8: cnr(3) was ready 3.4 us earlier than counted, 1.6 by units of 2.42 to 2.8, mostly less than the 2.7 I took, 1.1 because the four jobs ended sooner and 0.7 by the job between; score(2,0) waited 0.5 for POOL and not 3.
- *Ends*: stage 3 -3.9 (forecast -5.0): the wait for exp(15) was 0.5 longer, and mix(14,1) waited 0.56 for a remainder that I had there in time. Stage 0 -1.6 for -3.9 and stage 6 -0.6 for -5.0: in each about 1.5 us are lost because I counted full clock behind the wait for exp(15), in stage 6 another 1.8 around waits of 0.69 and 0.65 ahead of and behind the first output products, which the sum had without a wait. The mix after the wait for exp(15) took 2.88 at 134.10 and 2.38 at 710.36, with a granted clock of 0.51 and 0.62 in the 3 us from there, against 1.69 at 1.00 in stage 3 (484.59), though stages 3 and 6 had waits of the same size ahead of it (1.79 and 0.56; 1.75 and 0.56). Whether the clock falls there is not told by the wait: kernels 4 and 13 have 1.65 and 1.68 in stage 0 after 0.89 and 1.04, and after 0.91 and 0.89.
- *Behind stage 6*: +3.5, put at nothing in the sum; no row of the kernel before pointed to it.
- *The two rules beside the sum.* The Trainium skill (Perfetto Trace Analysis, Optimizing Scalar/DVE Operations) warns that moving work between these engines may not help because of the port they share. The runs bear it out in part: the move itself cost 4 us in stage 3 (kernel 6 against 2), and DVE's being kept out 10 (kernel 14 against 13). The Trainium skill (SBUF, State Buffer, SBUF: two separate sides) gives the port to whoever starts first; kernels 5 and 12 agree up to the 14th POOL instruction in a row, and kernel 12 shows that from the 15th DVE waits for the whole run. Its note that this concerns DVE's instructions with two inputs from SBUF agrees with kernel 5: an operand in PSUM left 0.74 as it was.

With L769 out of the way the sum is nearly met: kernel 2 has 1495.1 where 1496 was forecast, though partly by luck, for the part behind the first product of stage 9 is 4 us shorter than the changed kernel's.

What stays open: what the "issue" waits of stage 9 are. They come at the same five instructions of the program, counted in TensorE's matmuls, and the full kernels differ in which of them come and how long they are: that part takes from 615.8 (kernel 3) to 623.0 us (kernel 10). Nothing here tests what they wait for. Open too is why the clock fell behind some of these end waits and not behind others of the same size.

## What to carry to other kernels

Count POOL's instructions between two of its gaps before cutting them into pieces: up to the 14th, POOL lets DVE in at the end of an instruction; from the 15th on, a one-element DVE instruction with two or three operands in SBUF can stand until POOL idles, and everything behind it. Best give DVE nothing of that kind beside POOL (an operand in PSUM, a reduction of two neighbours, or ACT's scale and bias); failing that, let POOL wait for itself every ten instructions or so, which costs about 0.12 us each (in kernel 12 a unit takes 2.84 with such a wait and 2.72 without). And judge an edit by the stage it is in: parts never touched moved by up to 7 us here.

## What the hardware showed that I had not expected

- The entry of DVE between POOL's instructions ends with the 15th in a row, by count and not by time: pieces of 0.68 us at 10.14 us, pieces of 1.22 us still open at 16.93 us, closed at 19.19. The longest wait seen was 22.55 us, by one instruction on 128 x 1.
- A pause of POOL of 0.08 us resets it (kernels 12 and 13); an entry of DVE does not (kernel 11, and stage 3 of the changed kernel).
- A small reduction over two neighbouring values is undisturbed by POOL (0.14 to 0.16 us), while a maximum of two operands took 1.20 on average [rows 3]. One operand is not always enough: L722 of the kernel before, 512 columns of bytes to bf16, took 0.42 with POOL idle and 2.61 beside it [rows 6].
